# A hybrid transformer kernel: row sort lists in rounded operands, constants built inside the stages, scores ahead of the scoring's turns

## The reference, cut to what matters

```python
x = x + attn(layernorm(x), w_qkv, w_out)      # 16 heads of 32, band of 128 keys back
x = x + ffn(layernorm(x), gate_w, w1, w2)     # 8 experts, top 2 by softmax of the logits
x = x + mamba(layernorm(x), ...)              # in_proj, conv, scan in blocks of 64, out_proj
x = x + ffn(layernorm(x), gate_w, w1, w2)
```

## Time and profile before

| | us |
|---|---|
| median of three runs | 1694.79 |
| the profiled execution, its own time | 1690.24 |
| its span, first to last instruction | 1688.4 |
| TensorE busy | 1516.6 (90%) |
| VectorE busy | 906.7 (54%) |
| ScalarE busy | 715.7 (42%) |
| GpSimd busy | 604.4 (36%) |

### The profile page before, as it was taken

The page is one execution under the profiler, slowest core; times in us unless marked ns, Lnnn a source line. Parts: engine busy times, 40 slices in busy tenths (PEclk is TensorE's granted clock), DMA queues, the critical chain, the costliest instruction groups (busy, mean ns, idle before and its releaser), DMA issues. The chain is left out here.

```text
span 1688.4 us, 33729 instructions
## 1 busy us (share of the span) xinstructions
PE 1516.6 (90%) x11806; PEld 1249.9 (74%) x11822; DVE 906.7 (54%) x2087; ACT 715.7 (42%) x1776; POOL 604.4 (36%) x469
## 2 busy tenths in 40 slices
PE   3999999998689999995899999999999868999997
PEld 3787887786578888985767677666776447888897
DVE  3676677776622224225687785877857652222222
ACT  2666666666122224322554455544445302222232
POOL 5564555555122334433232223322223302333342
PEclk9999999999689999997999999999999968999999
DMA  5264454454559777533010101101000136787643
GB/s 207 88 207 145 173 199 158 165 188 169 184 188 337 195 228 208 117 62 90 14 33 20 51 20 33 32 20 47 24 20 20 32 125 207 232 238 223 186 88 57
DMA packets 94476, 212.34 MB, mean 126 GB/s; under 512 B 7184, under 2 KB 7184, under 8 KB 92944
## 3 DMA queue, kind: packets, MB, share of 16 engines
q1 hardware_dynamic: 76736, 166.58, 28.2%
q0 software_dynamic: 17472, 40.90, 12.1%
q10 hardware_dynamic: 144, 3.15, 0.5%
HBM read 136.94 MB, written 73.66 MB: 125 GB/s over the span
## 5 line engine op out<-in xcount | busy, mean ns | idle before, releaser
L1261 PE MATMUL bank<-ring,halves 128*128 x1872 | 336.2, 329 | 3.5 <-ACT halves L1110 3.5
L1261 PEld LDWEIGHTS bank<-ring,halves 128*128 128x128 f32 x1872 | 307.0, 191 | 11.2 <-issue 4.8
L498 POOL TENSOR_TENSOR arena<-arena 128x1024 f32<-128x1024 f32 x64 | 123.9, 1936 | 146.6 <-DVE arena L574 145.0
L1655 DVE SCALAR_TENSOR_TENSOR arena<-arena 128x256 f32<-128x256 f32 x240 | 146.1, 651 | 18.6 <-ACT arena L1857 15.8
L1120 ACT ACTIVATE arena<-bank 128x512 f32<-128x512 f32 x78 | 46.7, 598 | 221.1 <-DMA out_dram<-arena 79.9
L700 ACT ACTIVATE arena<-arena 128x256 f32<-128x256 f32 x256 | 126.4, 500 | 1.1 <-DVE arena L566 1.1
L779 PE MATMUL bank<-arena 128*128 128x128 f32 x1024 | 124.9, 281 | 1.7 <-ACT arena L681 0.8
L1084 POOL DMA_INDIRECT arena<-normalised_rows,arena x78 | 80.3, 1030 | 125.1 <-DVE arena L1213 56.9
L779 PEld LDWEIGHTS bank<-arena 128*128 128x128 f32 x1024 | 118.9, 195 | 7.6 <-issue 2.6
L1546 POOL TENSOR_TENSOR arena<-arena 128x1024 f32<-128x1024 f32 x16 | 31.3, 1959 | 249.3 <-ACT arena L1908 227.9
L2107 PE MATMUL bank<-arena 128*128 128x512 f32 x256 | 117.0, 611 | 1.2 <-ACT arena L1901 1.2
(11 more groups left out here) (263 smaller groups left out, 3184.0 us busy)
## 6 DMA issues: line engine op xcount, KB each, us to landing
ring<-expert_halves SPq DMA_DIRECT2D x16, 4352.0 KB
expert_halves<-expert_high SPq DMA_DIRECT2D x16, 1088.0 KB, 8.5
expert_halves<-expert_rest SPq DMA_DIRECT2D x16, 1088.0 KB, 10.7
arena<-in_w_dram SPq DMA_DIRECT2D x8, 1088.0 KB, 6.5
normalised_rows<-arena SPq DMA_DIRECT2D x33, 256.0 KB, 2.0
...
```

Source lines behind the costliest of these rows:

```text
L498: nc.gpsimd.tensor_tensor(held, held, spread(rinv[:, HG * g:HG * g + HG], 2, 2 * P), ALU.mult)\
L1261: last = nc.tensor.matmul(bank[1 + 2 * par + part][:, 0:INTER], rows_parts[a][:, par, k * P:k * P + P], weights(at, b, (2 * k + part) * IN ...
L1655: last = nc.vector.scalar_tensor_tensor(out=slot[:, j], in0=cin[:, c, k:k + PAIR], scalar=taps[:, c, k:k + 1], in1=slot[:, j], op0=ALU.mul ...
```

## The change

`make_constants` goes. What it built is made in three places on GpSimd, memsets included: nine operations at the start of attention (`first_constants`), five between the loop and the last two steps of attention (`sort_constants`), and nineteen at the start of the first expert stage (`mamba_constants`). VectorE keeps three memsets at the start of attention; the spare rows' stores take the zeros from `xo`. The weights for query, key and value come in three loads from ScalarE's queue; TensorE waits for each where it first uses it; the output weights are loaded after the value weights have landed, and x for the residual and the gate after them. ScalarE splits the value weights after the evictions of queries and keys. VectorE takes the second tile's statistics ahead of the mask.

In the step of attention on TensorE the scores of the second half come ahead of the scoring's turn.

In the sort, `at_spot` and `by_slot` are written in fp32r; the weight is split in a high part and a rest, so that `by_slot` has three columns a slot, with 40 slots; the product is one rounded pass over 120 columns. The table `one_hot` has one buffer instead of two. The weight's operations move from ahead of the tables to behind the choice, the gap ahead of the index search, and the spots of the last two tiles behind the first part of the tables. Two operations split the weight, one adds its two parts at the end. In mamba the sort's tiles lie elsewhere in the arena.

```diff
-def make_constants(core, spare_rows, w_qkv):
...
+def first_constants(core, g):
...
-        @block.sync
-        def _(sp):
-            sp.wait_ge(base_made, 1)
-            for rows in spare_rows:
-                sp.dma_start(rows, zero_rows).then_inc(zeroed, 16)
-            sp.wait_ge(zeroed, 16 * len(spare_rows))
-
-        @block.scalar
-        def _(act):
-            act.dma_start(core.wqkv, w_qkv).then_inc(core.w_qkv_in, 16)
...
+    g(nc.gpsimd.memset(core.ident[:], 0.0))
+    g(nc.gpsimd.affine_select(out=core.ident[:], in_=core.ident[:], compare_op=ALU.not_equal, fill=1.0, base=0,
+                              pattern=[[-1, P]], channel_multiplier=1))
+    g(nc.gpsimd.memset(core.att_mask[:], 0.0))
+    for which, own, prev in ((0, 0, None), (1, 0, 1), (2, 1, 0)):
+        m = core.att_mask[:, which, own * P:own * P + P]
+        g(nc.gpsimd.affine_select(out=m, in_=m, compare_op=ALU.is_ge, fill=NEG, base=0,
+                                  pattern=[[-1, P]], channel_multiplier=1))
+        if prev is not None:
+            m = core.att_mask[:, which, prev * P:prev * P + P]
+            g(nc.gpsimd.affine_select(out=m, in_=m, compare_op=ALU.is_ge, fill=NEG, base=0,
+                                      pattern=[[1, P]], channel_multiplier=-1))
+    g(nc.gpsimd.memset(core.att_mask[:, 0, P:2 * P], NEG))
+
+
+def sort_constants(core, g):
+
+    nc = core.nc
+    g(nc.gpsimd.memset(core.onesb[:], 1.0))
+    g(nc.gpsimd.affine_select(out=core.before[:], in_=core.onesb[:], compare_op=ALU.is_gt, fill=0.0, base=0,
+                              pattern=[[1, P]], channel_multiplier=-1))
+    g(nc.gpsimd.iota(core.count[:], [[1, P]], 0, 0, allow_small_or_imprecise_dtypes=True))
+    g(nc.gpsimd.iota(core.rowid[:], [[P, TILES]], 1, 1, allow_small_or_imprecise_dtypes=True))
+    g(nc.gpsimd.iota(core.spareid[:], [[0, 1]], ROWS + 1, 1, allow_small_or_imprecise_dtypes=True))
...
+def mamba_constants(core, g):
+
+    nc = core.nc
+    for ap, value in ((core.identb, 0.0), (core.ssd_mask, 0.0), (core.ones, 1.0), (core.in_block, 1.0), (core.keep, 1.0)):
+        g(nc.gpsimd.memset(ap[:], value))
+    g(nc.gpsimd.memset(core.keep[:, 0:1], 0.0))
+    g(nc.gpsimd.affine_select(out=core.identb[:], in_=core.identb[:], compare_op=ALU.not_equal, fill=1.0, base=0,
+                              pattern=[[-1, P]], channel_multiplier=1))
...
+def attention(core, x_in, x_out, xn_rows, w_out, gate, w1_dram, w2_dram, w2_tail, w_split, w_qkv, spare_rows):
...
         @block.sync
         def _(sp):
             for par in range(2):
                 sp.dma_start(x[:, par], x_in[par]).then_inc(x_loaded[par], 16)
+            sp.wait_ge(base_made, 1)
+            for rows in spare_rows:
+                sp.dma_start(rows, xo).then_inc(zeroed, 16)
+            sp.wait_ge(w_v_in, 16)
+            sp.dma_start(wo, w_out).then_inc(w_out_in, 16)
             for par in range(2):
                 sp.dma_start(xres[:, par], x_in[par]).then_inc(again_loaded[par], 16)
             sp.dma_start(core.gate[:], gate).then_inc(gate_in, 16)
-            sp.dma_start(wo, w_out).then_inc(w_out_in, 16)
 
             def one(t):
                 return slice(t, t + 1) if isinstance(t, int) else bass.ds(t, 1)
...
         def _(pool):
-            nc.gpsimd.memset(v, 0.0).then_inc(cleared, 1)
+            g = Chain(pool, made)
...
 
+            first_constants(core, g)
+            pool.wait_ge(base_made, 1)
             norm_power(0)
+            nc.gpsimd.memset(v, 0.0).then_inc(cleared, 1)
             norm_power(1)
             split_rows(0)
...
+            sort_constants(core, g)
             step(TILES - 2, True, load=False)
...
                 if sorting:
+                    dve.wait_ge(made, SORT_MADE)
                     sort.early_choice(link)
                 if front:
...
 
+            nc.vector.memset(core.zero[:], 0.0)
+            nc.vector.memset(core.mhalf[:], -0.5)
+            nc.vector.memset(xo, 0.0).then_inc(base_made, 1)
             nc.vector.memset(whole[LAST_I:P, 1, HALF - D:HALF], 0.0).then_inc(cleared, 1)
             nc.vector.memset(k_keys, 0.0).then_inc(cleared, 1)
             link = Chain(dve, chains[0])
             statistics(link, 0, 0, 0)
             normalise(0, 0)
+            statistics(link, 1, 1, 0)
+            dve.wait_ge(made, FIRST_MADE)
             pick_mask(0)
-            statistics(link, 1, 1, 0)
             dve.wait_ge(wv_split, 1)
             nc.vector.tensor_tensor(wv_parts[1], wqkv[:, :, 2 * D:3 * D], wv_parts[0], ALU.subtract)\
                 .then_inc(wv_split, 1)
             normalise(1, 1)
+            dve.wait_ge(zeroed, 16 * len(spare_rows))
             scores_out(0, 0, 0, 0)
             sums_out(0, 0)
             sums_out(0, 1)
...
 
+            for j, loaded in enumerate((w_q_in, w_k_in, w_v_in)):
+                act.dma_start(wqkv[:, :, j * D:j * D + D], w_qkv[:, :, j * D:j * D + D]).then_inc(loaded, 16)
             rows_out(0)
-            act.wait_ge(core.w_qkv_in, 16)
-            nc.scalar.activation(wv_parts[0], wqkv[:, :, 2 * D:3 * D], ACT.Copy).then_inc(wv_split, 1)
             act.wait_ge(cleared, 3)
             queries_out(0, 0)
             keys_out(0, 0)
+            act.wait_ge(w_v_in, 16)
+            nc.scalar.activation(wv_parts[0], wqkv[:, :, 2 * D:3 * D], ACT.Copy).then_inc(wv_split, 1)
             new_values_out(0, 0)
             exponentials(0, 0)
             exponentials(0, 1)
...
             def step(t, par, first=False, front=True):
                 begun = not (isinstance(t, int) and t < 2)
                 turn_probs(t, 0)
+                scores(t, 1, par)
                 if begun:
                     pe.wait_ge(v_ready, t + 1)
                     scored.turn(pe, t - 2, proj)
-                scores(t, 1, par)
                 values(t, 0)
                 if front:
...
 
-            pe.wait_ge(core.w_qkv_in, 16)
+            pe.wait_ge(made, 2)
             turn_rows(0)
+            pe.wait_ge(w_q_in, 16)
             queries(0)
+            pe.wait_ge(w_k_in, 16)
             keys(0)
             scores(0, 0, 0)
             pe.wait_ge(wv_split, 2)
...
+        self.one_hot, at = cut(arena, at, K * T // 4, SLOTS + 1)
+        self.empty = self.one_hot[:, 0, 0:SLOTS]
...
+        at = -(-at // 8) * 8
+        self.at_spot = rounded(core, f"{tag}_at_spot", at, K, T, P)
+        at += K * T * P
+        self.by_slot = rounded(core, f"{tag}_by_slot", at, K * T, 3, SLOTS + 1)
+        self.w_parts = rounded(core, f"{tag}_w_high", at + 3 * K * T * (SLOTS + 1), K, T)
+        at += 3 * K * T * (SLOTS + 1) + K * T
         assert at <= end, at - end
...
             step = nc.vector.max(self.best[:, t], logits[:, t])
         link(step)
+        if behind_maxima is not None:
+            behind_maxima()
...
+            if in_w is not None:
+                mamba_constants(core, Chain(pool, const_made))
             pool.wait_ge(index_ready, 1)
             for s in range(4):
...
                 E, T, K, N = EXPERTS, TILES, TOPK, sort.EARLY
-                sort.choose(link, N, T, both_ready)
-                nc.vector.tensor_tensor(sort.gap, sort.best[:, :, 1], sort.best[:, :, 0], ALU.subtract)\
-                    .then_inc(gap_ready, 1)
+
+                def gaps():
+                    nc.vector.tensor_tensor(sort.gap, sort.best[:, :, 1], sort.best[:, :, 0], ALU.subtract)\
+                        .then_inc(gap_ready, 1)
+
+                sort.choose(link, N, T, both_ready, gaps)
+                dve.wait_ge(exp_ready, 1)
+                link(nc.vector.tensor_scalar(sort.den, sort.gap_exp, 1.0, None, ALU.add))
+                link(nc.vector.reciprocal(sort.w[:, 0], sort.den))
+                link(nc.vector.tensor_tensor(sort.w[:, 1], sort.gap_exp, sort.w[:, 0], ALU.mult))
...
                 sort.ranks(link, N, T, rank_bank[:, 0:2 * E])
-                for k in range(K):
-                    last = sort.spots(N, T, k)
-                link(last)
                 link(nc.vector.tensor_tensor(sort.picked.rearrange("p k t e -> p (k t) e"),
                                              sort.chosen.rearrange("p k t e -> p (k t) e"),
                                              spread(sort.start, 1, K * T), ALU.mult))
                 link(nc.vector.tensor_reduce(sort.place, sort.picked.rearrange("p k t e -> p (k t) e"), AX.X, ALU.add))
                 link(nc.vector.tensor_tensor(sort.place, sort.place, sort.full.rearrange("p k t -> p (k t)"), ALU.add))
-                dve.wait_ge(exp_ready, 1)
-                link(nc.vector.tensor_scalar(sort.den, sort.gap_exp, 1.0, None, ALU.add))
-                link(nc.vector.reciprocal(sort.w[:, 0], sort.den))
-                link(nc.vector.tensor_tensor(sort.w[:, 1], sort.gap_exp, sort.w[:, 0], ALU.mult))
+                link(nc.vector.tensor_copy(sort.w_parts, sort.w[:, 0:K]))
+                link(nc.vector.tensor_tensor(sort.w[:, K:2 * K], sort.w[:, 0:K], sort.w_parts, ALU.subtract))
```

(28 more changed lines are left out.)

97 lines of the change are left out of this document (31 added, 66 removed).

## The result

The changed kernel took 1667.97 us (median, 1665.24 to 1677.63); the kernel before, beside it on the same chip, 1695.27 (1694.64 to 1696.12). The ratio is 0.9849, 95% interval 0.9807 to 0.989: faster, by 27.3 us on the medians (18.6 to 32.7 by the interval). The profiled execution took 1665.86 (span 1664.1) against 1690.24 (1688.4), so 24.3 us is what the two traces can explain. The other 3.0 come from where the profiled executions stand among their runs: 5.0 us under the median before, 2.1 under it after. The sum in the prediction was 22.3, its time 1672.5.

A forecast was written before the change was run, and what follows sets the result against it. TensorE, busy nine tenths of the span, was taken as the bound, leaving few holes; 5.0 + 6.0 + 5.0 + 6.3 = 22.3 us off the median 1694.79 made 1672.5 us, range 1663 to 1683.5.

The forecast's parts named there:

- The forecast case: Whole kernel: the prediction's own forecast, 22.3 us off, 1672.5 us; chance 0.60.
- Start: Start of attention: without the stage of constants, queries and exponentials start sooner; gain 5 us, bounds 3 to 9.
- VectorE first: Start: VectorE's value-weight rest precedes GpSimd's subtraction, second normalisation waits for GpSimd; exponentials near 30.1, gain 7 us.
- The other branch: Start: GpSimd's output-weight subtraction comes first and holds VectorE's value-weight rest; exponentials at 33.8, gain 3.3 us.
- Steps: Attention steps: scores ahead of turns fill TensorE's hole; 0.45 us a step in 13 steps, 6.0 us in all.
- Rival 2: Attention steps: ScalarE's later turned rows, with VectorE's copies behind GpSimd, eat the gain; 6 us lost, 1678.5; chance 0.08.
- rival 3: Attention: the start gains the whole 9 us and the steps 9, giving 1665.5 us; chance 0.10.
- Lists: Both sorts: one rounded record of 218 ns a product, VectorE's tables bounding; gain 6.3 us second sort, 5.0 first.
- rival 1: Sorts' lists: narrow rounded operands pay four cycles a column; gain 1.5 instead of 6.3 a sort, 1682 us; chance 0.16.
- Rival 5: Sorts' lists: VectorE's tables bound them more than counted; 16 us lost in both sorts, 1688.5 us; chance 0.03.
- rival 4: Attention steps: later turns push ScalarE's evictions and lengthen each step; 1.7 us a step gives 1700 us; chance 0.03.
- the prediction's own sign of being wrong: Mamba stage or experts' slots: a change over 2 us would show the prediction wrong, since nothing there was edited.

The follow-up runs named there:

- e6b: Changed kernel with GpSimd's split of the output weights held back until VectorE's second normalisation is through: 1667.91 us, ratio to the kernel before 0.9858.
- e4: Changed kernel with the second tile's normalisation ahead of the rest of the value weights on VectorE: 1670.63 us, ratio to the kernel before 0.9863.
- e3: Changed kernel with the scan's constants built behind the second gather of the first experts instead of ahead of the gathers: 1664.83 us, ratio 0.9848.
- e9: Changed kernel with ScalarE's eviction of the next rows ahead of its expert split in the attention step: 1667.46 us, ratio to the kernel before 0.9854.
- e1: Changed kernel with only the moved scores undone, the scoring's turn ahead of them again: 1680.24 us, ratio to the kernel before 0.9908.
- e7: Changed kernel with the lists' operands in true fp32 again, three columns kept: 1673.41 us, ratio to the kernel before 0.989.
- e5: Changed kernel with the second normalisation ahead of the value weights' rest and the first exponentials ahead of the copy of new values: 1667.3 us, ratio 0.9829.
- e8: Changed kernel without the lists' column for the weights' rest, so the experts' weights are only rounded: 1666.67 us, ratio to the kernel before 0.9863.

## Why the prediction was right

The forecast case came, and its four terms lie 1.7, 0.5, 0.3 and 0.1 us from what the traces show. Nothing in the order of its mechanisms had to be turned round but one wait. What it put at nothing did not stay so, though: the mamba stage is 6.0 us longer in these traces, which a gain of 4.3 in the first experts hid.

**Start** (5 forecast, 6.7 measured; mis-sized within its bounds). Queries at 8.75 against 8.5; VectorE's statistics at 3.62 against 4.2, with most of the difference lost in the first normalisation. The output weights were issued at 15.17, since v landed at 15.16, 1.6 us past the 13.5 that I scaled from one transfer of 3 MB. I had counted x ahead of v, but not the three stores of zeros: issued at 1.72 to 2.96, they landed at 9.22 to 11.96, ahead of v, where before they had been issued behind the weights and landed behind them. That delay made GpSimd the later one (20.31 for 19.0), so the branch "VectorE first" came, which the prediction put at 30.1: measured 30.44. The wait is the one it named, the second normalisation and the scores behind it (28.96 for 28.6). What it did not price in this branch is the value product at 1.2 GHz, which would have let the exponentials start only 0.2 us sooner, so that e6b, which took the wait away, gained 0.85 us and not 5. The other branch it put at 33.8, and e4 and e3 show it at 33.70 and 34.55. The 5 was a value between two branches that no execution has; 7, the branch that came in seven of the eight traces with this start, would have been the better forecast.

The Trainium skill (SBUF — State Buffer, on the shared port pair) has GpSimd and VectorE shut each other out for a whole instruction, for VectorE's operations with two inputs in SBUF and for its fast modes, which a `tensor_scalar` like the normalisation can enter. The traces agree: 0.54 against 4.76 us for the normalisation, 2.29 against 6.14 and 6.50 for the rest, which both times ended 2.1 to 2.2 us behind the end of GpSimd's subtraction. For the constants in the first sort the 1.3 stood for 0.95, nearer to the lower bound; that most of the selects last 0.3 us and meet operations of 0.17 fits this, but was not tested.

**Steps** (6.0, measured 6.5): right in size, incomplete in what holds them. The prediction had ScalarE's queue as the limit, 0.25 us later with its 0.72 of slack gone. That chain came as forecast, the row eviction 4.63 us behind the probability turns' weight load (216.29 - 211.66 forecast, 207.45 - 202.82 measured) and without idle time before it. But e9 took it out of the way and nothing moved. The step that failed is about VectorE's copies, 0.25 late: "that is hidden behind the same ScalarE chain". They are a wait of their own: VectorE ends the normalisation (L209, 202.64 to 204.76) and copies behind it, and TensorE's values (L841) wait for them, with the turn of the rows behind them in its queue: 0.33 of the 0.78 us is given back. The two chains end within 0.05 us of each other, so either way of counting gives about 0.45 a step, by chance. Rival 2 (nothing gained) and rival 3's 9 us in the steps both fell with e1's 7.3.

**Lists** (6.3 and 5.0, measured 6.2 and 5.3). One pass, no four cycles a column: rival 1 fell. The pitch was 229 ns and not 218, which with the 0.57 us hole makes TensorE end 0.1 us later than summed; VectorE's tables at 1.86 were forecast at 1.88. The Trainium skill (FP8 and Floating Point Precision, on FP32 at reduced precision) has four passes for true FP32 only; 229 ns at 1.2 GHz for 120 columns agree, since four passes would take 400. What the expectation of e7 took for given, that 120 columns in fp32 run at 0.50 to their end, did not come. Rival 5, tables that bound the lists by more, fell with their 1.86 us; rival 4, longer steps, with the 0.44 us by which each step got shorter. The prediction also counted rival 5 as "same", though its 1688.5 is 6.3 us under 1694.79 and so outside the 3.4 that it named.

**Outside the edits** the stretch between the sorts grew by 1.7 us and the last one shrank by 1.4, both under the 2 us that would have counted against me. But the first of these numbers is the sum of two larger ones. From the first sort's indices to the end of the first experts' last product it is 288.99 us before and 284.69 after, 4.3 less; that part scatters, 282.6 to 291.2 over the changed kernel and its eleven variants. From there to the second sort's maxima, the mamba stage, it is 615.3 us before and 621.4 after, 6.0 more, and 620.3 to 623.5 in all twelve traces. So the prediction's own sign of being wrong, a mamba stage changed by more than 2 us, did come.

About 4.5 of the 6.0 is TensorE's clock. From one scoring turn to the next, every second step of the mamba loop lasts 33.8 us in the changed kernel; in the kernel before the first three of them last 32.2, 32.2 and 32.5. The same place in the first of these steps, 5.1 us behind the turn, before and after:

```profile
871.50:875.50 4.00, 4.00 (x35) 3.78 (x35) 1.85 (x4) 3.35 (x7) 0.00 (x0) 1.00 0.00 0
```

```profile
850.40:854.40 4.00, 4.00 (x29) 3.91 (x29) 1.44 (x3) 2.64 (x5) 0.00 (x0) 0.69 0.02 4
```

In the next two such steps it is the same: 1.00 throughout before, down to 0.50 after. Two of the variants (e5, e8) have one step of 32.2 as well, so it is not the edit alone that decides. There is one trace of the kernel before, and whether the moved code and tiles of the mamba stage cost these 6 us or another execution of the kernel before would show them too stays open.
